# A convolution and patch-spectrum kernel: image rows in two buffers, patch rows in five

## What is computed

```
x = x + _L0_conv_ref(_gn(x), ...)     # depthwise 3x3 with weights chosen per image, then 32 -> 32 channels
x = x + _L1_conv_ref(_gn(x), ...)
# _L1_conv_ref:
hidden = einsum('oc,bchw->bohw', w_hidden, x)          # 32 -> 192 channels
hidden = depthwise 3x3 of hidden
q, k, v = split(hidden, 3)                             # 64 channels each
out = irfft2(rfft2(8x8 patches of q) * rfft2(8x8 patches of k))
out_norm = (out - mean over channels) / sqrt(var + 1e-5) * norm_w + norm_b
return einsum('oc,bchw->bohw', w_out, v * out_norm)    # 64 -> 32 channels
```

## Time and profile before

| | |
|---|---|
| median of three runs | 2265.87 us (2260.75 to 2266.81) |
| the profiled execution: its time, its span | 2273.27 us, 2271.2 us |
| busy in the span: TensorE, VectorE, ScalarE, GpSimd | 94%, 77%, 63%, 23% |
| stage 1, up to about 505 us; stage 2 from there | 505 us; 1766 us |
| TensorE's mean granted clock | 0.971 of 2.4 GHz |

### The profile page before, as it was taken

One profiled execution on the slowest core, in us unless ns is written; L12 is line 12 of the kernel. 1 busy time (PEld: TensorE's weight loads), 2 busy tenths in 40 slices (PEclk: granted clock), 3 DMA queues, 4 the chain that ended last, 5 costly groups with the idle time before them and its releaser, 6 DMA issues.

```text
span 2271.2 us, 101012 instructions
## 1 busy us (share of the span) xinstructions
PE 2145.7 (94%) x45303; PEld 1364.8 (60%) x45303; DVE 1741.6 (77%) x4186; ACT 1432.6 (63%) x2629; POOL 517.1 (23%) x323
## 2 busy tenths in 40 slices
PE   6888888977999999999999999999999999999997
PEld 3333333336666666666666666666666666666664
DVE  4666666645888888888888888788888888878886
ACT  3456655656666666666666666666666666666662
POOL 1000000000332222322222222233322322322222
PEclk9989988888999999999999999999999999999998
DMA  7688888876333333333333333333433333333312
GB/s 144 163 220 224 223 219 219 207 193 157 79 83 84 79 90 86 79 78 79 79 79 81 85 83 79 83 88 79 97 85 82 88 79 88 79 78 79 79 40 57
DMA packets 60386, 248.21 MB, mean 109 GB/s; under 512 B 12393, under 2 KB 12658, under 8 KB 53810
## 3 DMA queue, kind: packets, MB, share of 16 engines
q1 hardware_dynamic: 59954, 241.75, 44.9%
HBM read 139.99 MB, written 101.72 MB: 106 GB/s over the span
## 4 chain that ended last, share of the span: by engine, by line
PE 90%; issue 4%; ACT 2%; DVE 2%; DMA 1%; POOL 0%; SPq 0%; POOLq 0%; ACTq 0%
PE bank L590 24%; PE bank L530 17%; PE bank L575 10%; PE bank L662 10%; PE bank L650 9%; PE bank L603 7%; PE bank L683 6%; PE bank L612 5%; DVE arena L1215 2%; ACT arena L826 1%; ACT arena L731 1%; DMA arena<-tap_rows_in 1%; PE bank L544 0%; ACT arena L817 0%; PE bank L492 0%
## 5 line engine op out<-in xcount | busy, mean ns | idle before, releaser
L459 POOL TENSOR_TENSOR arena<-arena 128x8 f32<-128x8 f32 x256 | 492.8, 1925 | 1238.0 <-DVE arena L1125 1235.5
L590 PE MATMUL bank<-arena 128*64 128x512 f16 x4608 | 690.2, 394 | 0.0
L817 ACT ACTIVATE arena<-bank 100x512 f32<-100x512 f32 x1024 | 581.8, 599 | 110.1 <-PE bank L575 79.4
L575 PEld LDWEIGHTS bank<-arena 128*64 128x64 f16 (+1 forms) x8192 | 328.7, 104 | 232.6 <-issue 22.3
L530 PE MATMUL bank<-arena 32*32 32x508 f32 (+1 forms) x9216 | 384.2, 655 | 51.1 <-issue 36.4
L575 PE MATMUL bank<-arena 128*64 128x128 f16 (+1 forms) x8192 | 389.3, 220 | 18.0 <-DVE arena L1109 11.5
L1215 DVE TENSOR_TENSOR arena<-bank,arena 128x512 f32<-128x512 f32 x512 | 328.9, 684 | 48.2 <-issue 44.9
L826 ACT ACTIVATE arena<-bank,arena 128x256 f32<-128x256 f32 x512 | 261.3, 561 | 114.1 <-PE bank L603 111.2
L859 ACT ACTIVATE arena<-bank 128x512 f32<-128x512 f32 x256 | 152.9, 597 | 225.7 <-PE bank L650 223.9
L1144 DVE TENSOR_TENSOR arena<-arena,bank 128x512 f32<-128x512 f32 x256 | 174.8, 683 | 139.6 <-ACT arena L826 139.6
L650 PE MATMUL bank<-arena 100*32 100x128 f32 x8192 | 276.1, 275 | 1.3 <-ACT arena L817 1.3
(11 more groups left out here) (113 smaller groups left out, 1655.9 us busy)
## 6 DMA issues: line engine op xcount, KB each, us to landing
arena<-xn_d SPq DMA_DIRECT2D x128, 536.2 KB, 4.8
xn_d<-arena SPq DMA_DIRECT2D x130, 260.0 KB, 4.4
x_d<-arena SPq DMA_DIRECT2D x64, 512.0 KB, 8.1
arena<-x_d SPq DMA_DIRECT2D x128, 256.0 KB, 4.1
out<-arena SPq DMA_DIRECT2D x128, 256.0 KB, 2.7
arena<-x_in SPq DMA_DIRECT2D x32, 544.0 KB, 9.6
arena<-x_in SPq DMA_DIRECT2D x32, 528.0 KB, 9.4
arena<-spectra_in SPq DMA_DIRECT2D x1, 384.0 KB
```

What stands on the lines that cost most here:

```text
L459: pool.tensor_tensor(tiny["rstd"][:, slot], tiny["var_eps"][:, slot], powers, ALU.pow).then_inc(s_root, 1)
L575: mm = pe.matmul(ring[g % len(ring)][low:high, 128 * i:128 * i + 128], w[:, first + low:first + high], hidden_w, start=True, stop=True)
L590: mm = pe.matmul(v_banks[chunk % 3][64 * s:64 * s + 64, :], v_w[:, 64 * tap:64 * tap + 64], at(xs[u % 3], row * WP + 32 * k + dx, [32 * WP ...
L817: act.activation(h_rows[0:WIN, :, first:first + 4], ring[g % len(ring)][0:WIN, :].rearrange("p (i c) -> p c i", i=4), ACT.Copy).then_inc(s ...
```

## The change

Two `xs` buffers in place of three (`xs[u % 2]`). The load of u + 1 now writes the buffer that u - 1 used, so it may begin only when all v chunks of u - 1 are done, and SP waits for `s_v_mm` 8u, which is T0, where it waited for the first hidden group of u. The load is cut in two: `load_top` brings rows 0 to 41 of 66 (four DMAs, each waited for) ahead of `store_res(u - 1)`, `load_bottom` rows 42 to 65 (four DMAs, waited for two by two) behind it and ahead of `load_res(u, 0)`. Each half has its own semaphores; window 0 waits for the top, window 5 for the bottom.

Five `win` buffers in place of three. Windows 0 to 4 of u + 1 are copied behind the last product of `spectral(u)`, windows 5 to 7 at p = 1, 2 and 3 of `front`; the two copies behind `scale(tail, 0)` and `scale(tail, 1)` are gone from there. At the start of stage 2, five windows stand ahead of the last statistics of stage 1 where three stood. Three small memsets of GpSimd and a wait for them go. TensorE's and ScalarE's order stays as it is.

```diff
-        s_xs_in = [semaphore(f"xs_in{s}") for s in range(3)]
+        s_top_in = [semaphore(f"top_in{s}") for s in range(2)]
+        s_bottom_in = [semaphore(f"bottom_in{s}") for s in range(2)]
...
-        xs = [take(HALF * WP, f16) for _ in range(2)] + [xs_late]
+        xs = [take(HALF * WP, f16) for _ in range(2)]
...
-        win = [take(1632, f16) for _ in range(3)]
+        win = [take(16 * WIN, f16) for _ in range(WINS)]
...
-            def load_xs(u, paced=True):
-
-                b, half = divmod(u, 2)
+            def load_xs(u, landed, first, last, at_once):
+
+                b, h = divmod(u, 2)
                 for g in range(4):
-                    src = xn_d[b, g % 2, :, half * (H // 2):half * (H // 2) + HALF, :].rearrange("c h w -> c (h w)")
-                    sp.dma_start(xs[u % 3][32 * g:32 * g + 32, :], src).then_inc(s_xs_in[u % 3], 16)
-                    if paced:
-                        sp.wait_ge(s_xs_in[u % 3], 64 * (u // 3) + 16 * (g + 1))
+                    src = xn_d[b, g % 2, :, h * (H // 2) + first:h * (H // 2) + last, :].rearrange("c h w -> c (h w)")
+                    sp.dma_start(xs[u % 2][32 * g:32 * g + 32, first * WP:last * WP], src).then_inc(landed[u % 2], 16)
+                    if (g + 1) % at_once == 0:
+                        sp.wait_ge(landed[u % 2], 64 * (u // 2) + 16 * (g + 1))
+
+            def load_top(u, at_once):
+                load_xs(u, s_top_in, 0, TOP, at_once)
+
+            def load_bottom(u, at_once):
+                load_xs(u, s_bottom_in, TOP, HALF, at_once)
...
                 if b == NB + 1:
-                    load_xs(1, paced=False)
+                    load_top(1, 8)
+                    load_bottom(1, 8)
...
             for u in range(1, LAST + 1):
+                sp.wait_ge(s_v_mm, 8 * u)
                 if u < LAST:
-                    sp.wait_ge(s_hidden_mm, 32 * u + 1)
-                    load_xs(u + 1)
+                    load_top(u + 1, 1)
                 store_res(u - 1)
+                if u < LAST:
+                    load_bottom(u + 1, 2)
                 sp.wait_ge(s_inverse_mm, 4 * u + 3)
                 load_res(u, 0)
...
             def window(u, r):
 
-                if positive(32 * u + 4 * (r - 2)):
-                    dve.wait_ge(s_hidden_mm, 32 * u + 4 * (r - 2))
+                if positive(32 * u + 4 * (r - WINS + 1)):
+                    dve.wait_ge(s_hidden_mm, 32 * u + 4 * (r - WINS + 1))
                 if r == 0:
-                    dve.wait_ge(s_xs_in[u % 3], 64 * (u // 3 + 1))
+                    dve.wait_ge(s_top_in[u % 2], 64 * (u // 2 + 1))
+                if r == TOP // 8:
+                    dve.wait_ge(s_bottom_in[u % 2], 64 * (u // 2 + 1))
...
             def front(u, tail):
-                rows = iter(range(3, 8) if u is not None else ())
+                rows = iter(range(5, 8) if u is not None else ())
...
                 scale(tail, 0)
-                windows()
                 centre(tail, 1)
                 pixel_stats(tail, 2)
                 variance(tail, 2)
                 scale(tail, 1)
-                windows()
...
                 if u < LAST:
-                    for r in range(3):
+                    for r in range(5):
                         window(u + 1, r)
```

More of the change, by code:

```diff
@@ L84, in build @@
     SUMS = 6
+    TOP = 42
+    WINS = 5
     def dram(name, shape, dt):
@@ L119, in build @@
         s_pool_consts = semaphore("pool_consts")
-        s_win_room = semaphore("win_room")
         s_prep = semaphore("prep")
@@ L287, in build @@
         res = take(2048)
-        xs_late = take(HALF * WP, f16)
         top[0] = max(top[0], stage1_end)
-        xs = [take(HALF * WP, f16) for _ in range(2)] + [xs_late]
+        xs = [take(HALF * WP, f16) for _ in range(2)]
         G_q = take(64 * 64)
         G_k = take(64 * 64)
-        win = [take(1632, f16) for _ in range(3)]
+        win = [take(16 * WIN, f16) for _ in range(WINS)]
         block = ctx.enter_context(nc.Block())
@@ L382, in _ @@
                     sp.wait_ge(s_pads_stored, 32)
-                    load_xs(0, paced=False)
+                    load_top(0, 8)
+                    load_bottom(0, 8)
             def image_rows(base, b, half, jr, s):
@@ L436, in _ @@
             pool.memset(xl.bitcast(f32), 0.0).then_inc(s_pads_zero, 1)
-            for s in range(3):
-                pool.memset(win[s][:, 16 * WIN:1632].bitcast(f32), 0.0).then_inc(s_win_room, 1)
             pool.wait_ge(s_pool_consts, 2)
             pool.wait_ge(s_pads_zero, 2)
-            pool.wait_ge(s_win_room, 3)
             for b in range(-1, NB + 1):
@@ L570, in hidden_group @@
                     pe.wait_ge(s_h_ready, 32 * u + g + 1 - len(ring))
-                w = win[(8 * u + g // 4) % 3]
+                w = win[(8 * u + g // 4) % WINS]
                 for i in range(4):
@@ L590, in v_chunk @@
                         mm = pe.matmul(v_banks[chunk % 3][64 * s:64 * s + 64, :], v_w[:, 64 * tap:64 * tap + 64],
-                                       at(xs[u % 3], row * WP + 32 * k + dx, [32 * WP, 2], [WP, 8], [1, 32]),
+                                       at(xs[u % 2], row * WP + 32 * k + dx, [32 * WP, 2], [WP, 8], [1, 32]),
                                        start=tap == 0, stop=tap == 8)
@@ L1103, in window @@
             def window(u, r):
-                if positive(32 * u + 4 * (r - 2)):
-                    dve.wait_ge(s_hidden_mm, 32 * u + 4 * (r - 2))
+                if positive(32 * u + 4 * (r - WINS + 1)):
+                    dve.wait_ge(s_hidden_mm, 32 * u + 4 * (r - WINS + 1))
                 if r == 0:
-                    dve.wait_ge(s_xs_in[u % 3], 64 * (u // 3 + 1))
-                dve.tensor_copy(win[(8 * u + r) % 3][:, 0:16 * WIN].rearrange("p (j y x) -> p j y x", y=10, x=10),
-                                     at(xs[u % 3], 8 * r * WP, [8, 16], [WP, 10], [1, 10])).then_inc(s_win_ready, 1)
+                    dve.wait_ge(s_top_in[u % 2], 64 * (u // 2 + 1))
+                if r == TOP // 8:
+                    dve.wait_ge(s_bottom_in[u % 2], 64 * (u // 2 + 1))
+                dve.tensor_copy(win[(8 * u + r) % WINS][:, 0:16 * WIN].rearrange("p (j y x) -> p j y x", y=10, x=10),
+                                     at(xs[u % 2], 8 * r * WP, [8, 16], [WP, 10], [1, 10])).then_inc(s_win_ready, 1)
             def pixel_stats(u, p):
@@ L1166, in front @@
                     shifts(NB + 2, NB - 1, None)
-                    windows(4)
+                    windows(2)
                     for i in range(4):
@@ L1224, in spectral @@
                 if u < LAST:
-                    for r in range(3):
+                    for r in range(5):
                         window(u + 1, r)
-            dve.wait_ge(s_win_room, 3)
-            for r in range(3):
+            for r in range(5):
                 window(0, r)
```

## The result

| | before | after |
|---|---|---|
| median of ten runs each, taken together | 2269.29 us (2260.75 to 2275.71) | 2284.27 us (2272.62 to 2295.49) |
| the profiled execution: its time, its span | 2273.27, 2271.2 us | 2282.71, 2280.8 us |
| TensorE's mean granted clock | 0.971 | 0.977 |

The changed kernel takes 1.0064 times as long, with an interval of 1.0036 to 1.0092: slower by 15 us. The direction was forecast and the time lies inside the range of 2262 to 2345 us, but 36.5 us were forecast: the size of the delay was not.

What follows compares the result with a forecast made beforehand. TensorE was taken to bound the kernel, with SP's lengthened queue delaying x2: 30 half-images at 1.2 us make 36 us, plus 0.5 at the start of stage 2, so 2265.9 + 36.5 = 2302 us, range 2262 to 2345.

Steps and rivals of the forecast that it cites:

- the price of late x2: VectorE's residual, then TensorE's project(u, 1), wait for x2: 1.2 us a half-image, 30 times, 36 us more.
- the queue's sum: SP's round from T0: reaction 0.1, top 15.4, store 11.9, bottom 8.5, x2 9.7; x2 lands at T0 + 45.6.
- 0.1 us for the scatter: Added to the 1.1 us delay of each half-image because SP's rounds scatter, mostly by the store; early rounds give nothing back.
- The bound: TensorE bounds the kernel: busy 94% of the span, 90% of the chain, so the change has next to nothing to take away.
- The limit: The residual may start at T0 + 44.5 before TensorE feels it; each microsecond later costs TensorE one.
- in time after all: Rival: SP's round ends by T0 + 44.5 if top and bottom take 1.1 us less; 2266 us (2260 to 2272), chance 0.15.
- duration rule: Each DMA takes about 2.0 us plus bytes at 436 GB/s: SP's round 39.5 us, in time by 5; given little weight.
- Size hardly matters: Rival: each top DMA takes 4.85, each bottom pair 4.84; round 50.8, late by 6.3; 2455 us; beyond 2350 has chance 0.06.
- faster: Rival: two copies out of front let TensorE run without its waits, 20 us over stage 2: 2246 us; under 2259 chance 0.03.
- The clock: TensorE's pauses of 1 to 3 us, once in 55 us, leave its clock at 1.00; nothing charged.
- The start of stage 2: Two more window copies, 1.0 us, ahead of the last statistics, once: +0.5 us, between -1 and +1.
- VectorE at window 5 first: Sign of being wrong: VectorE stands at window 5 before the residual; the bottom was to land 1.3 us ahead of window 5.

Runs made afterwards that it cites:

- second profile: The changed kernel run once more unedited, for another profile: one run, 2277.16 us; its 30 half-images took 1632.1 us against 1630.7.
- e1_loads_alone: Changed kernel with the window copies put back where they were (three buffers), loads as changed: median 2288.6 us, 1.0092 times the kernel before.
- e7_top_halves: Changed kernel with each top DMA split by rows into two of 21 rows (5,460 B), issued together: one run, 2290.95 us.
- e6_one_dma_more: Changed kernel with one more 256 KB DMA of x2 issued and waited for ahead of the load of x2, u = 1 to 30: one run, 2373.85 us.
- e5_whole_at_once: Changed kernel with all 66 rows loaded at T0 by four 536 KB DMAs, one by one, no bottom load: 2304.84 us, ratio 1.0161.

## Where the prediction was right, and which step failed

**The step that failed** is the price of late x2, the last term of the queue's sum: "1.2 us a half-image", in all 30 of them, 36 us. It rests on a sum for the round that was 1.3 us too long (T0 + 45.6 for 44.3) and on 0.1 us for the scatter. The runs showed x2 late in eight of 30 half-images, for 9.3 us (nine and 12.0 in the second profile). A second term was put at nothing without a reason: what the moved load does to the work beside it, 5 to 6 us. The 17.9 us of the half-images are 9.8 for x2, 5.3 more of spectral part than before, and 2.7 more of rest. The parts follow.

**The bound and the queue's mechanism: right.** TensorE bounds both kernels, nothing is gained by the windows, and SP's new round puts x2 at the edge of its deadline. The limit holds too. I had T0 + 44.5; the traces give 44.6. With that limit the sum of max(0, landing - 44.6 - spectral delay) over the 30 half-images is 9.3, 12.0, 13.3, 17.3 and 85.1 us for the two profiles of the changed kernel, e1_loads_alone, e7_top_halves and e6_one_dma_more. The x2 parts measured are 9.8, 12.2, 13.9, 17.4 and 85.5; in the changed kernel the surplus of 0.5 is the short pauses at u = 3 and 4.

**The sum of the round: the term that was mis-sized.** Forecast and measured means, in us:

| step | forecast | measured |
|---|---|---|
| top, with the reaction | 15.5 | 14.9 |
| store | 11.9 | 12.0 |
| bottom | 8.5 | 7.7 |
| x2 | 9.7 | 9.7 |
| x2 landed | T0 + 45.6 | T0 + 44.3 |

The fastest rows with 0.005 us a KB gave 3.6 us for a top DMA; for the median I took 3.85, which is 0.25 more where the rows had 0.2. It took 3.7. For the bottom I took the pair of x2 less 122 KB, and the pair of 195 KB came out 0.4 us shorter than that. Together 1.3 us of 45.6, 3% of the sum. But the sum ends within a microsecond of the limit, so this 3% moved the mean from 1.0 beyond it to 0.3 ahead of it. Then the mean costs nothing and the scatter is all: eight of 30 half-images are late, by 0.1 to 2.9 us, and not all 30 by 1.2. My allowance of 0.1 for scatter was right for a sum well beyond the limit and wrong for one at it. The cost against the mean landing runs 42.2: 0.9 us, 44.3: 9.8, 44.4: 13.9, 44.9: 17.4, 47.6: 85.5. A straight line from 44.9 to 47.6 (some 25 us for 1 us) gives 36 at my 45.6, so the price of a landing beyond the limit was right. With the right landing, though, my rule would have charged the 0.1 for scatter alone, 3 us, and not the 9.3 to 12.0 that the scatter cost. (Two slips changed little: the store's own terms add up to 11.8 and not 11.9, and the upper end of the range to 47.5 and not 47.3.)

**The rival "in time after all"** had its condition met on the mean: it asked top and bottom together for 1.1 us less, and they took 1.4 less, with a top DMA of 3.7 and a shorter bottom. Its time, 2266 us, was wrong all the same, since it put nothing on the scatter or on the spectral part; "each store that lands late breaks it" is what happened. Its duration rule from the Trainium skill, "DMA: Bandwidth & Descriptors", section "Anatomy of one DMA", would have the top DMAs at 2.8 us and the round at 39.5; the rows have 3.7 and 44.3, so the rule, fitted for DMAs issued by GpSimd, is too short for these, as the earlier trace rows had said. "Size hardly matters" is out: 341 KB takes 3.7 and 536 KB takes 4.8. So is "faster".

**The spectral part: not foreseen.** I asked of the moved load only when it would end, and not what it would run beside. Before, the load lay in the stretch of the hidden groups, where the 536 KB DMAs did no harm that the period shows; now it lies beside the q and k transforms, and costs 5 to 6 us. In the forecast this step was costed at nothing without being named. That it is smaller than the error of the queue term is luck: e5_whole_at_once shows 34 us for a load in the same place. It is luck too that the time lies nearer to the forecast than the queue term does: the spectral part (5.3) and the rest (2.7, of which the clock 1.6), both put at nothing, made up for 8 of the 26 us that x2 cost less than forecast.

**The clock: right for short pauses, wrong for the longest.** The changed kernel has one half-image in which it matters, u = 30. VectorE and TensorE there, and then stretches of the core (start:end, length, busy per engine, clock, DMA share, GB/s):

```profile
2202.55 0.69 DVE L1161 TENSOR_TENSOR arena<-bank,arena 128x512 f32<-128x512 f32 x1 [3.25 <-DMA arena<-x_d]
...
2203.29 2.06 PE L620 MATMUL bank<-arena 128*64 128x512 f32 x4 [2.21 <-DVE arena L1161]
...
2201.00:2204.00 3.00, 0.79 (x7) 0.30 (x4) 1.45 (x4) 0.63 (x2) 0.00 (x0) 1.00 0.01 4
2205.00:2207.00 2.00, 2.00 (x9) 1.07 (x10) 1.60 (x3) 0.56 (x2) 1.79 (x1) 0.50 0.00 0
2208.00:2213.00 5.00, 5.00 (x72) 3.04 (x68) 4.32 (x11) 3.84 (x7) 1.95 (x1) 1.00 0.00 0
```

By the measure above project(u, 1) was 2.86 us late. The granted clock is at 2.4 GHz (1.00) from 2201 to 2204, at 1.2 (0.50) from 2205 to 2207, and at 2.4 again from 2208 on, and the half-image lost 1.6 us more. Over all profiles, a delay of up to 2.65 us cost some 0.15 more, one of 2.7 or more cost 1.1 to 2.3 more. In e6_one_dma_more 15 of 30 half-images crossed that, which is its rest of 25.5 us. The granted clock bears it out: it is at 1.2 GHz for a while in just these 15 half-images and in none of the other 15, and in the changed kernel in u = 30 alone. The earlier trace rows had a pause of 2.38 us at full clock, and I read it as "pauses cost no clock"; it said so only up to its own length.

**The small terms.** The start of stage 2, forecast at +0.5 within -1 to +1, is neutral: from the last convolution of stage 1 to T0 of u = 1 it takes 88.5 us, 88.7 before. SP's first load of a round is at T0 + 0.04. "VectorE at window 5 first" was to prove me wrong: window 5 was late by itself once, in u = 30, by 0.7 us, with the bottom just in (SP went on to x2 at T0 + 37.79, window 5 started at 37.87); the wait at the residual behind it was longer.

## What to carry to other kernels

When a serial queue ends near a deadline that renews itself every round, its cost is the mean of max(0, landing minus limit) over the scatter of the rounds: work out mean and scatter apart, and expect a microsecond of error in a long sum to decide the result; the waits between its DMAs are the first thing to give up (here x2 came in 7 us sooner without them). Ask of a load that is moved not only when it lands but beside which work it will run; beside dense matmuls try it in rows of some 5 KB a partition, which here took most of its cost away at the same bytes (from 6.1 to 2.0 us and from 34.4 to 3.8).

## What the runs showed of the hardware

- Packets of 10,920 B beside TensorE's transforms cost 5 to 6 us in 30 half-images when the DMAs go one at a time and 19 us when they go in pairs, and packets of 17,160 B cost 34 us; packets of 5,460 and 5,720 B cost 2.0 and 3.8 us, no load at all 2.5. That the code's packets stand behind those of the load is the reading that fits, not shown; what is shown is that all 71 unexplained pauses of TensorE end 2.2 to 3.1 us behind the start of a 16 KB packet of the "instruction" queue.
- Medians from issue to landing: reads of HBM into 32 partitions issued by SP landed in 3.2 us for 195 KB (two at a time), 3.7 for 341 KB and 4.8 for 536 KB (one at a time).
- A pause of TensorE that made a half-image 2.7 us or more late was followed by a few microseconds at 1.2 GHz and cost 1.1 to 2.3 us beyond itself (15 of 30 half-images of e6_one_dma_more); where it was up to 2.65 us late, the clock stayed at 2.4 GHz and 0.15 to 0.2 more was the most.
